# Twenty products of the identity between the own-key scores and the third turn's scores of a second cross-attention

## The reference, cut to what matters

```python
def _L1_xattn_ref(x, context, w_qkv, w_proj, b_proj):
    H, D = 16, 16
    qkv = (x @ w_qkv.T).reshape(B, N, 3, H, D).transpose(2, 0, 3, 1, 4)
    q, k, v = (qkv[0], qkv[1], qkv[2])
    kv = context.reshape(B, N_c, 2, H, D).transpose(2, 0, 3, 1, 4)
    k = jnp.concatenate([kv[0], k], axis=2)      # 1024 context keys, then the 64 own keys
    v = jnp.concatenate([kv[1], v], axis=2)
    attn = jax.nn.softmax(jnp.einsum('bhnd,bhmd->bhnm', q * D ** -0.5, k), axis=-1)
    out = jnp.einsum('bhnm,bhmd->bhnd', attn, v)
    return out.transpose(0, 2, 1, 3).reshape(B, N, C) @ w_proj.T + b_proj
```

## Time and profile before

| | us |
|---|---|
| median of 3 runs | 493.35 |
| lowest and highest run | 491.14 and 494.48 |
| the profiled execution | 493.21 |
| span of its profile, first to last instruction | 491.2 |
| mean granted TensorE clock, share of full speed | 0.986 |

### The profile page before, as it was taken

The page is one execution under the profiler, slowest core; times in us unless marked ns, Lnnn a source line. Parts: engine busy times, 40 slices in busy tenths (PEclk is TensorE's granted clock), DMA queues, the critical chain, the costliest instruction groups (busy, mean ns, idle before and its releaser), DMA issues.

```text
span 491.2 us, 8735 instructions
## 1 busy us (share of the span) xinstructions
PE 468.0 (95%) x3630; PEld 398.7 (81%) x3630; DVE 266.0 (54%) x461; ACT 238.7 (49%) x423; POOL 109.4 (22%) x101
## 2 busy tenths in 40 slices
PE   8998999999999999999879899988999899889997
PEld 7887989898988999899766669974666798778697
DVE  2657132345345141420357979855676465469896
ACT  2576332454446151430137876716688262237772
POOL 1120000011000000000113848783000000019695
PEclk9999999999999999999999999995899999999999
DMA  8925400016000200000299999960000093164000
GB/s 282 406 69 182 172 1 1 1 38 219 1 1 0 80 8 0 2 1 1 85 424 357 280 330 418 408 272 1 1 1 2 7 402 113 82 256 173 0 1 12
DMA packets 13080, 62.53 MB, mean 127 GB/s; under 512 B 1296, under 2 KB 3728, under 8 KB 7281
## 3 DMA queue, kind: packets, MB, share of 16 engines
q1 hardware_dynamic: 11024, 54.27, 29.6%
q0 software_dynamic: 2016, 7.70, 4.5%
HBM read 61.84 MB, written 0.13 MB: 126 GB/s over the span
## 4 chain that ended last, share of the span: by engine, by line
PE 79%; DVE 9%; ACT 5%; issue 3%; POOL 3%; DMA 0%; DVEq 0%; ACTq 0%; POOLq 0%
PE W L1414 19%; PE W L1370 15%; PE W L1579 9%; PE W L1630 8%; PE W L1703 4%; PE W L1670 4%; PE W L1387 3%; PE W L1720 2%; POOL w_lo L535 2%; PE W L1436 2%; PE W L1293 2%; PE W L1322 1%; POOL small L544 1%; PE W L1653 1%; PE W L1571 1%
## 5 line engine op out<-in xcount | busy, mean ns | idle before, releaser
L1414 PE MATMUL W<-probs_turned_hi,ctx_split_hi 128*128 128x256 f32 x256 | 72.8, 285 | 2.5 <-issue 2.5
L1414 PE MATMUL W<-probs_turned_hi,ctx_split_lo 128*128 128x256 f32 x256 | 72.4, 283 | 0.0
L1414 PE MATMUL W<-probs_turned_lo,ctx_split_hi 128*128 128x256 f32 x256 | 72.4, 283 | 0.0
L544 POOL TENSOR_TENSOR small<-small,const 128x1 f32<-128x1 f32 (+2 forms) x10 | 7.0, 696 | 238.7 <-DVE small L997 122.1
L924 DVE TENSOR_TENSOR probs_turned_lo<-W,probs_turned_hi 128x512 fp32r<-128x512 f32 x32 | 20.6, 686 | 64.9 <-ACT probs_turned_hi L644 64.9
L1414 PEld LDWEIGHTS W<-probs_turned_hi,ctx_split_hi 128*128 128x128 f32 x256 | 49.1, 192 | 3.7 <-issue 3.3
L1630 PE MATMUL W<-w_hi,acts 128*128 128x256 f32 x272 | 49.9, 285 | 1.0 <-DVE acts L896 1.0
L535 POOL TENSOR_TENSOR w_lo<-arena,w_hi 128x320 fp32r<-128x320 f32 x32 | 42.1, 1329 | 33.0 <-ACT w_hi L586 32.9
L1414 PEld LDWEIGHTS W<-probs_turned_lo,ctx_split_hi 128*128 128x128 f32 x256 | 49.1, 192 | 0.2
L1414 PEld LDWEIGHTS W<-probs_turned_hi,ctx_split_lo 128*128 128x128 f32 x256 | 49.1, 192 | 0.0
L889 DVE TENSOR_TENSOR w_lo<-arena,w_hi 128x704 fp32r<-128x704 f32 (+1 forms) x36 | 46.1, 1318 | 4.7 <-ACT w_hi L586 4.3
(11 more groups left out here) (367 smaller groups left out, 900.6 us busy)
## 6 DMA issues: line engine op xcount, KB each, us to landing
arena<-units_dram SPq DMA_DIRECT2D x22, 1024.0 KB, 11.9
ctxmem<-units_dram SPq DMA_DIRECT2D x16, 1024.0 KB, 14.1
fixed<-units_dram SPq DMA_DIRECT2D x6, 1024.0 KB, 6.0
pbuf<-ctx_dram POOLq DMA_DIRECT2D x4, 512.0 KB, 6.5
ctxmem<-ctxT_dram SPq DMA_DIRECT2D x8, 256.0 KB, 12.1
ctxmem<-ctx_dram SPq DMA_DIRECT2D x2, 1024.0 KB, 16.0
scr<-ctx_dram POOLq DMA_DIRECT2D x3, 512.0 KB, 4.5
vecs<-vectors_dram POOLq DMA_DIRECT2D x1, 1040.0 KB, 8.0
```

What stands on the lines that cost most here:

```text
L1414: mm = pe.matmul(ps, CXN[a][:, t, c * P:(c + 1) * P], PT[z][:, t, :], start=(t == 0 and n == 0), stop=(t == KEYT - 1 and n == 2))
```

## The change

Between the own-key scores and the definition of the turns, PE waits until DVE has copied the own-key scores of the first batch, then multiplies the identity by itself twenty times into bank 4:

```diff
                 mm.then_inc(ev("self_ps"), 1)
 
+            pe.wait_ge(ev("self_sb"), 1)
+            stay_warm(4, 20)
+
             def turn1(r):
 
                 pe.wait_ge(ev("exp1_done"), r + 1)
```

## The result

The changed kernel takes 489.86 us (median of 7 runs, 487.74 to 491.31) against 493.72 us (7 runs, 491.14 to 495.19): a ratio of 0.9937, with a 95% interval of 0.991 to 0.9964. Between the medians that is 3.9 us, 0.8%; the ratio, which is not that of the two medians, says 0.6%. Both are inside the 1% that the prediction called no change to tell. The predicted 489.2 us is 0.7 us from the measured median. The profiled execution is the one of 489.86 us, with a span of 487.9 us.

A forecast was written before the change was run, and what follows sets the result against it. The prediction blamed PE's 13.66 us half-speed stretch after an idle wait: +2.3 us for products, -6.45 us returned, -4.15 us in sum, giving 489.2 us; forecast bounds 489.0 to 490.4, 8-in-10 range 487.6 to 494.2.

The forecast's parts named there:

- the 1% that the prediction called no change to tell: Whole kernel: one per cent, 4.9 us, is about what a measurement can tell from no change.
- The wait at 0 us: PE's added wait for DVE's copy of the first own-key scores is over before PE arrives: 0 us.
- The products at 4.45 us: Twenty products, 40 instructions, behind the own-key scores: 4.45 us, the first 2.15 us hidden in PE's wait.
- I take it to stay up: PE's clock stays at full speed after the added products, from 331 to 348 us, removing the 13.66 us half-speed stretch.
- predicted 4.15: Net gain by the sixth turn's scores: 2.3 us later start against 6.45 us returned by the clock, 4.15 us.
- There is no other half-speed stretch: Kernel before: the 13.66 us at 1.2 GHz, 333.86 to 347.52, accounts for the mean clock's whole gap to full.
- 8.11 us for the eight pieces at full clock: Third to sixth turn's scores: three groups of scores, three of transposes, two of values take 8.11 us, not 14.56.
- 0.8 us in hand at the fifth turn: Fifth turn's scores are due at 340.55, the third softmax they need is ready at 339.75: 0.8 us spare.
- Rival one: Clock falls at 333.9 all the same, from the thin products ahead of the wait; 495.5 us, chance 0.08.
- Rival two: Clock falls later, in the scores and transposes from 335.4 to 339.8 without values' products; 494 us, chance 0.12.
- Rival three: Last block: gain partly lost because expert weights are split no earlier; half lost gives 491.2 us, chance 0.05.
- the 2.3 us past the pause: Products outlast PE's wait, so the third turn's scores start at 335.4 instead of 333.12: 2.3 us later.

The follow-up runs named there:

- e1: Changed kernel with the wait alone, the twenty products removed; 493.32 us, ratio 1.0021 to the kernel before.
- e5: Changed kernel with forty transposes of the identity in place of the twenty products; 489.28 us, ratio 0.993 to the kernel before.
- e4: The changed kernel again, no edit, for a second trace; 489.78 us, ratio 0.9951 to the kernel before.
- e6: Changed kernel with 40 more thin own-key products (32 rows deep, 80 instructions) in place of the twenty products; 497.18 us, ratio 1.0081 to the kernel before.
- e8: Changed kernel with five products in place of twenty; 490.08 us median of 4 runs, two near 486 and two near 494.
- e7: Changed kernel with PE first waiting for the first turn's softmax, then the twenty products; 493.04 us, ratio 1.0017 to the kernel before.
- e2: Changed kernel with nine products in place of twenty; 487.39 us, ratio 0.9911 to the kernel before.
- e10: Changed kernel without wait and twenty products, only five products ahead of the second turn's scores; 489.16 us, ratio 0.9944 to the kernel before.
- e9: Changed kernel with five products ahead of the second turn's scores and five behind the own-key scores, replacing the twenty; 486.67 us, ratio 0.9891 to the kernel before.
- e12: The kernel of e9 run once more, for more runs; 488.00 us, ratio 0.9877 to the kernel before.

## Why the prediction was right, and where it was not

*The wait at 0 us*: right (e1, 1.0021 with 1 inside the interval).

*The products at 4.45 us*: right where the clock is 1.00 (4.52 in e5 for as many instructions), 4.69 at 0.95. Where the clock has fallen they cost 6.16 us (e4), which the term did not allow for. (40 x 0.112 is 4.48; the slip changes nothing.)

*"I take it to stay up"* is the step that failed. In one of the two traces of the changed kernel the clock still falls, now at the end of the thin products, and the dense ones bring it back after 3.4 us; 15 of 18 runs have such a stretch somewhere by their mean clocks, and how many of them have it here is not shown. A run without a dip gains 4.1 us in the stage (e5, predicted 4.15); e4's gains 20.39 - 18.05 = 2.3 (327.38 to 345.43). The forecast for the median, 4.1, stood for the first kind. That the first medians differ by 3.9 is in part luck: they include both kinds, and a kernel before that itself varied from 489 to 495 us, with about 8 to 24 us at half speed by mean clocks of 0.992 to 0.975 in all but one of its recorded runs. Beside the 12 runs of e4 the gain is 2.9 us, and the ratios, 0.9937 and 0.9951, say 3.1 and 2.4 us.

*"There is no other half-speed stretch"*: wrong. The trace of before starts slowly too, under a clock shown as 1.00 (last section), which the change does not touch.

*8.11 us for the eight pieces at full clock*: in e4 337.31 to 345.43 is 8.12 us. The 0.8 us in hand at the fifth turn were there.

*Rival one* had a cause that the runs bear out and the wrong price. The clock does fall during the last thin products with no pause before it (e1, e4, e6, e8), but the rival let the half speed last until 347.5 as before, when dense products end it early (e4, e7). My argument against its cause, that the clock stood at 1.00 during those thin products, was a bad one: in those executions too it stood at 1.00 through most of them and fell at 330.5 to 331.2, during the last of them.

*Rival two* is refuted by e5, and by e4, where the stretch of scores and transposes alone (337.31 to 341.69) ran at 1.00.

*Rival three*: refuted. From the sixth turn's scores to the last block's long piece are 464.94 - 347.68 = 117.26 us before and 462.69 - 345.43 = 117.26 in e4. Nothing downstream took any of it back.

*Not weighed at all*: that fewer products would do. The prediction priced the 2.3 us past the pause and stopped there; with nine they are saved (e2).

What stays open is how the pause and the thin products share the blame in the kernel before. In e1, alike but for the wait, the clock fell before the pause; in the trace of before it fell 0.7 us behind it; in e10 a fall follows a pause of 0.7 us after fewer thin products. A pause behind dense work alone was not tried.

## What to carry to other kernels

Work that only fills a wait should fit the wait: the part of it that runs past (here 2.3 us of 4.5) is paid in full. Ask what stands ahead of a wait, not only how long it is: products that use a quarter of the rows looked busy in the profile and did not hold the clock here, and with five dense ones among them and five behind twelve of twelve runs had a mean clock of 1.000, against three of eighteen with twenty behind. Look at the mean clock of every run before trusting one trace, and at the length of like products where the clock itself may be shown wrongly: the kernel before and e1, alike but for a wait that costs nothing, lost the clock at 333.9 and at 330.5 us and for 13.7 and 17.1 us.

## What the runs showed of the hardware that I had not expected

A clock of 0.95 over nearly all of one execution (489.86 us), seen in one of the 19 runs of the changed kernel; one run of the kernel before, beside e5 to e8, reads 0.937 (494.87 us). In the first of them plain fp32 transposes took 1.16 us for nine in place of 1.13 and scores 1.09 in place of 1.06, while the last block's fp32r products took 23.53 us against 23.55: these rows did not slow with it.

Runs of e9 and e12 at a clock of 1.000 still fall into two groups, 486.2 to 486.8 and 487.8 to 488.2 us. The mean clock hides what most likely parts them, a slow start. The same six identity products near the start, in e9 (488.00 us) and in e5 (487.76 us, of the lower of the two groups of e5 at 1.000):

```profile
6.08 1.65 PE L1293 MATMUL W<-const 128*128 128x128 f32 x6 [0.46 <-ACT xT L579]
6.15 0.94 PE L1293 MATMUL W<-const 128*128 128x128 f32 x6 [0.46 <-ACT xT L579]
```

The clock is shown as 1.00 for both, but the trace's own clock records begin only at 10.0 us in e9 and at 6.0 in e5, and 1.65 to 0.94 is about what half and full clock make of such a group elsewhere (ten such instructions take 2.50 us in e8 at 0.50 and 1.38 in e9 at 1.00). The products of L1347 then start at 12.38 us in e9 and at 10.79 in e5, 1.6 us apart. All fourteen traces have 1.65 or 0.94 us here, and it is the execution that decides, not the kernel: the changed kernel has 0.94 in its first trace and 1.65 in e4; the kernel before has 1.65. Both kept traces of e9 and e12 are of the upper group and start slowly; of the lower group no trace was kept, so for these runs the cause is not shown.
